# Part of the first tile's results that the adapters give: first half two row tiles on, second half behind the second tile's p7

## What is computed

```python
x = x + (x @ W.T + b + (x @ sign) * coeff)                # sign = 2*mask - 1, one matrix per batch
gate = x @ W_gate.T + 0.5 * (x @ A_gate[i].T) @ B_gate[i].T   # i: adapter of the batch
up   = x @ W_up.T   + 0.5 * (x @ A_up[i].T)   @ B_up[i].T
act  = silu(gate) * up
x = x + act @ W_down.T + 0.5 * (act @ A_down[i].T) @ B_down[i].T
```

## Time and profile before

| | us |
|---|---|
| median of 3 runs | 1600.77 |
| lowest and highest | 1599.63, 1600.84 |
| the profiled execution, its own time | 1599.98 |
| its span | 1598.2 |
| TensorE busy | 1557.8 (97%) |
| VectorE busy | 1219.1 (76%) |
| ScalarE busy | 803.0 (50%) |
| GpSimd busy | 355.3 (22%) |

### The profile page before, as it was taken

One profiled execution on the slowest core, in us unless ns is written; L12 is line 12 of the kernel. 1 busy time (PEld: TensorE's weight loads), 2 busy tenths in 40 slices (PEclk: granted clock), 3 DMA queues, 4 the chain that ended last, 5 costly groups with the idle time before them and its releaser, 6 DMA issues.

```text
span 1598.2 us, 23033 instructions
## 1 busy us (share of the span) xinstructions
PE 1557.8 (97%) x7508; PEld 1308.6 (82%) x7508; DVE 1219.1 (76%) x2134; ACT 803.0 (50%) x1478; POOL 355.3 (22%) x677
## 2 busy tenths in 40 slices
PE   6999998999999999999999989999999999999999
PEld 6999976888888888878888868888888888778887
DVE  8999877676666666688888877767666666788886
ACT  8999855444444444443334464444444444433332
POOL 0000131222222222253410012222212123543100
PEclk9999999999999999999999999999999999999999
DMA  9999853444444444698593724443444445996653
GB/s 371 373 363 364 302 177 125 139 138 155 143 136 155 155 155 155 224 352 270 182 370 111 239 83 155 155 144 122 151 151 143 133 152 175 337 343 209 224 192 118
DMA packets 137350, 325.24 MB, mean 204 GB/s; under 512 B 20112, under 2 KB 43792, under 8 KB 137232
## 3 DMA queue, kind: packets, MB, share of 16 engines
q0 software_dynamic: 56608, 175.81, 33.2%
q1 hardware_dynamic: 76016, 139.57, 25.8%
q10 hardware_dynamic: 4608, 8.39, 1.4%
HBM read 233.51 MB, written 90.18 MB: 203 GB/s over the span
## 4 chain that ended last, share of the span: by engine, by line
PE 90%; DVE 6%; issue 2%; ACT 1%; DMA 1%; POOL 0%; SPq 0%; DVEq 0%; POOLq 0%; ACTq 0%
PE ps L1447 60%; PE ps L1443 27%; PE ps L1571 2%; DVE acc L1088 1%; DVE op_b L1085 1%; DVE lo L1085 1%; DVE raw L1085 0%; DMA b_in<-in_b_gu 0%; DVE fx L1085 0%; DMA x_scratch<-x_out 0%; DMA ident_sb<-in_ident 0%; ACT t_gate L751 0%; POOL b_in L639 0%; DVE g L1088 0%; DVE raw L1088 0%
## 5 line engine op out<-in xcount | busy, mean ns | idle before, releaser
L1447 PE MATMUL ps<-op_b,hi 128*128 128x512 f32 x1616 | 500.8, 391 | 4.7 <-ACT ps L751 4.7
L1085 DVE TENSOR_TENSOR lo<-raw,hi 128x512 fp32r<-128x512 f32 (+2 forms) x640 | 332.7, 529 | 132.5 <-ACT hi L751 130.5
L751 ACT ACTIVATE hi<-raw 128x512 fp32r<-128x512 f32 (+1 forms) x592 | 304.5, 518 | 213.3 <-PE ps L1447 175.3
L1447 PEld LDWEIGHTS ps<-op_b,hi 128*128 128x128 f32 x1616 | 304.9, 189 | 70.4 <-ACT ps L751 5.6
L1447 PE MATMUL ps<-op_b,lo 128*128 128x512 f32 x808 | 316.8, 392 | 0.0
L1447 PE MATMUL ps<-op_d,hi 128*128 128x512 f32 x800 | 248.8, 392 | 8.5 <-DVE acc L1088 8.3
L1443 PE MATMUL ps<-op_b,hi 128*128 128x512 f32 x816 | 254.5, 393 | 0.0
L626 POOL DMA_DIRECT2D operand_scratch<-ot x140 | 75.7, 541 | 640.7 <-DVE ot L1085 605.7
L1088 DVE TENSOR_TENSOR acc<-acc,ps 128x512 f32<-128x512 f32 x248 | 169.7, 684 | 54.1 <-PE ps L1447 47.5
L1447 PEld LDWEIGHTS ps<-op_d,hi 128*128 128x128 f32 x800 | 147.8, 188 | 44.5 <-DVE acc L1088 14.3
L1443 PEld LDWEIGHTS ps<-op_b,hi 128*128 128x128 f32 x816 | 154.3, 189 | 33.7
(11 more groups left out here) (120 smaller groups left out, 2220.5 us busy)
## 6 DMA issues: line engine op xcount, KB each, us to landing
operand_scratch<-ot POOLq DMA_DIRECT2D x140, 512.0 KB, 3.9
op_d<-operand_scratch POOLq DMA_DIRECT2D x140, 512.0 KB, 10.8
raw<-in_wgu SPq DMA_DIRECT2D x168, 256.0 KB, 4.3
m_raw<-in_mask SPq DMA_DIRECT2D x64, 512.0 KB, 5.5
raw<-in_wd SPq DMA_DIRECT2D x160, 128.0 KB, 4.4
w_in<-in_w SPq DMA_DIRECT2D x32, 512.0 KB, 6.3
b_in<-in_b_gu POOLq DMA_DIRECT2D x264, 32.0 KB, 2.4
x_scratch<-x_out POOLq DMA_DIRECT2D x32, 256.0 KB, 4.8
```

The lines of the kernel that those rows point to most:

```text
L751: return nc.scalar.activation(o, i, ACT.Copy)
L1085: return nc.vector.tensor_tensor(o, a, b, ALU.subtract)
L1447: return mm(dst, weight, v, start=False, stop=stop, skip_group_check=True)
```

## The change

TensorE's order: r(0) moves from before h(1,4) to before h(1,6), and r(1) from before p3 of tile 1 to behind p7; td(0) moves from before p2 to behind it. The steps of ScalarE and VectorE follow: half 0's result comes after the first t4 form; t low of half 1 comes before the forms t3, `lora_b` of tile 1 goes out of `first_result` to the place before the last t3 form, and t neg goes behind the result. `lora_b` of tile 0 writes its weights into t_neg's tile (`b_first`), whose place is free until then, so that those of tile 1 need not wait for r. Both halves' gates use g1, with the counts of `silu_count` in the new order, and p3 of tile 1 waits for t_ready on TensorE by itself.

```diff
--- before.py
+++ after.py
@@ -71,17 +71,16 @@
             ("ta", 0, 1): a_part(0, 4) + forms("b22", 2, 3) + [("make", 0)],
             ("ta", 0, 3): a_part(0, 6) + [("make", 1)] + forms("t1", 0),
             ("ta", 0, 5): a_part(1, 0) + [("make", 2)] + forms("t1", 1),
-            ("ta", 0, 7): a_part(1, 2) + [("lora_b",), ("t sum", 0), ("make", 3)] + forms("t1", 2)
+            ("ta", 0, 7): a_part(1, 2) + [("lora_b", 0), ("t sum", 0), ("make", 3)] + forms("t1", 2)
                           + [("t own", 0), ("t high", 0), ("t low", 0)] + forms("t1", 3),
             ("ta", 1, 1): a_part(1, 4) + forms("t2", 0, 1, 2, 3),
             ("ta", 1, 3): a_part(1, 6),
+            ("h", 1, 5): [("make4", 0), ("make4", 1)] + forms("t4", 0),
             ("r", 0): [("result", 0)],
-            ("h", 1, 5): [("make4", 0), ("make4", 1)] + forms("t4", 0),
             ("h", 1, 6): [("make4", 2), ("make4", 3)] + forms("t4", 1, 2, 3),
             ("ta", 1, 7): [("t sum", 1)] + forms("t3", 0) + [("t own", 1)],
-            ("g", 1, "p1"): [("t high", 1)] + forms("t3", 1) + [("t low", 1)] + forms("t3", 2, 3),
-            ("r", 1): [("result", 1)],
-            ("g", 1, "p3"): [("t neg",)]}
+            ("g", 1, "p1"): [("t high", 1), ("t low", 1)] + forms("t3", 1, 2) + [("lora_b", 1)] + forms("t3", 3),
+            ("r", 1): [("result", 1), ("t neg",)]}
 
 
 def first_stage_order():
@@ -97,11 +96,10 @@
         for o in range(KQ, HT):
             order += [("h", s, 0, o)] + [("ta", s, 0, 2 * (o - KQ) + i) for i in range(2)]
         for o in range(HT):
-            if o == KQ:
+            if o == KQ + 2:
                 order += [("r", s, 0)]
             order += [("h", s, 1, o), ("ta", s, 1, o)]
-        order += [("g", s, 1, u) for u in PRODUCTS[:3]] + [("r", s, 1)]
-        order += [("g", s, 1, u) for u in PRODUCTS[3:5]] + [("td", s, 0)] + [("g", s, 1, u) for u in PRODUCTS[5:]]
+        order += [("g", s, 1, u) for u in PRODUCTS[:5]] + [("r", s, 1), ("g", s, 1, "p2"), ("td", s, 0), ("g", s, 1, "p4")]
         for f in range(2, PAIRS):
             order += [("g", s, f, u) for u in PRODUCTS[:4]] + [("td", s, f - 1)]
             order += [("g", s, f, u) for u in PRODUCTS[4:]]
@@ -272,6 +270,7 @@
                 t_gate = [sb(gate, f"t_gate{h}", [TR, N], f32r) for h in range(HALVES)]
                 t_up = [sb(gate, f"t_up{h}", [TR, N], f32r) for h in range(HALVES)]
                 t_neg = sb(gate, "t_neg", [TR, N], f32r)
+                b_first = t_neg[:, :].rearrange("p (a n) -> p a n", n=P)
                 b_w = sb(gate, "b_w", [TR, 2 * HALVES, P], f32r)
                 lw = sb(gate, "lw", [P, LW_RING, P], f32r)
                 b_in0 = sb(gate, "b_in0", [TR, 2 * HALVES, 2 * P], f32)
@@ -365,7 +364,8 @@
 
         def silu_count(s, f, half):
 
-            return s * (PAIRS * 2 + 2) + 2 * f + (1 + half if f in (0, PAIRS) else 2 - half)
+            turn = {(0, 1): 3, (1, 1): 2}.get((f, half), 2 * f + (1 + half if f in (0, PAIRS) else 2 - half))
+            return s * (PAIRS * 2 + 2) + turn
 
         a_count = silu_count
 
@@ -823,11 +823,9 @@
                 act.wait_ge(b_loaded[c % 2], 16 * 12 * b_turn(s, c))
                 if f > 1:
                     act.wait_ge(pe_done, done["g", s, f - 1, "p4"])
-                elif f:
-                    act.wait_ge(pe_done, done["r", s, 1])
-                elif s:
-                    act.wait_ge(pe_done, last_left(s - 1))
-                copy(b_w[:, :, :], b_in[c % 2][:, :, f % 2 * P:(f % 2 + 1) * P]).then_inc(bw_h, 1)
+                else:
+                    act.wait_ge(pe_done, done["h", s, 0, 0])
+                copy((b_w if f else b_first)[:, :, :], b_in[c % 2][:, :, f % 2 * P:(f % 2 + 1) * P]).then_inc(bw_h, 1)
 
             def prep(key):
                 if plan.slot_free[key]:
@@ -888,17 +886,13 @@
                     copy(dst[R2:2 * R2, :], u2[r:r + R2, :]).then_inc(t_hi, 1)
 
             def t_gu_neg(s):
+                act.wait_ge(pe_done, done["r", s, 1])
                 act.wait_ge(t_ready, 4 * s + 4)
                 nc.scalar.activation(t_neg[:, :], t_up[1][:, :], ACT.Copy, scale=-1.0).then_inc(t_neg_ready, 1)
 
             def first_result(s, half):
-                if half:
-                    lora_b(s, 1)
                 act.wait_ge(pe_done, done["r", s, half])
-                gate = (g1, g2)[half]
-                if half:
-                    act.wait_ge(t_ready, 4 * s + 4)
-                nc.scalar.activation(gate[:, :], first_bank(0, half)[:, :], ACT.Silu).then_inc(silu_made, 1)
+                nc.scalar.activation(g1[:, :], first_bank(0, half)[:, :], ACT.Silu).then_inc(silu_made, 1)
                 act.wait_ge(form_l, form_count(s, *(("t3", KQ - 1) if half else ("t1", 1))))
                 act.wait_ge(a_made, a_count(s, 0, half))
                 operand_hi((s, 0, ("b11", "b12")[half]), a32[:, half, :])
@@ -976,7 +970,7 @@
                             act.wait_ge(tm, tm_count(s, f // 2 - 1, name))
                             operand_hi((s, f // 2 - 1, name), src)
                 elif u == "p2":
-                    act.wait_ge(a_made, a_count(s, f - 1, 0))
+                    act.wait_ge(a_made, a_count(s, f - 1, int(f == 1)))
                     nc.scalar.activation(g1[:, :], ps[3 * (f % 2) + 2][:, :], ACT.Silu).then_inc(silu_made, 1)
                     act.wait_ge(a_made, a_count(s, f, 1))
                     operand_hi((s, f // 2, ("b12", "b22")[f % 2]), odd_or_even(f))
@@ -1050,7 +1044,7 @@
                     elif kind == "lw":
                         lora_a(("ta", s, *args))
                     elif kind == "lora_b":
-                        lora_b(s, 0)
+                        lora_b(s, *args)
                     elif kind == "t sum":
                         t_gu_sum(s, *args)
                     elif kind == "t own":
@@ -1150,8 +1144,8 @@
 
             def lora_b(s, f):
                 dve.wait_ge(bw_h, s * FT + f + 1)
-                q = slice(R2, 2 * R2)
-                sub(b_w[q, :, :], b_in[f // 2 % 2][q, :, f % 2 * P:(f % 2 + 1) * P], b_w[q, :, :]).then_inc(bw_l, 1)
+                q, tile = slice(R2, 2 * R2), b_w if f else b_first
+                sub(tile[q, :, :], b_in[f // 2 % 2][q, :, f % 2 * P:(f % 2 + 1) * P], tile[q, :, :]).then_inc(bw_l, 1)
 
             def raw_in(g, name):
                 cell, turn = plan.load_turn[g, name]
@@ -1225,11 +1219,10 @@
 
             def first_result(s, half):
                 if half:
-                    lora_b(s, 1)
                     dve.wait_ge(form_l, form_count(s, "t3", KQ - 1))
                 dve.wait_ge(pe_done, done["r", s, half])
                 dve.wait_ge(silu_made, silu_count(s, 0, half))
-                mult(a32[:, half, :], (g1, g2)[half][:, :], first_bank(1, half)[:, :]).then_inc(a_made, 1)
+                mult(a32[:, half, :], g1[:, :], first_bank(1, half)[:, :]).then_inc(a_made, 1)
                 operand_lo((s, 0, ("b11", "b12")[half]), a32[:, half, :])
                 if half:
                     dve.wait_ge(a_made, a_count(s, 0, 1))
@@ -1273,7 +1266,10 @@
                 elif u == "p3":
                     dve.wait_ge(pe_done, done[key])
                     dve.wait_ge(copied, copy_count(s, f, "p6"))
-                    dve.wait_ge(a_made, a_count(s, f - 1, int(f == 1)))
+                    if f == 1:
+                        dve.wait_ge(ta_own, 4 * (s + 1))
+                    else:
+                        dve.wait_ge(a_made, a_count(s, f - 1, 0))
                     add(g2[:, :], u2c[:, :], y_ps[:, :]).then_inc(c_made, 1)
                 elif u == "p7":
                     dve.wait_ge(pe_done, done[key])
@@ -1487,7 +1483,7 @@
                 pe.wait_ge(bw_l, s * FT + 1)
                 pe.wait_ge(t_ready, 4 * s + 2 * half + 2)
                 for row, t in enumerate((t_gate[half], t_up[half])):
-                    end = mm_on(first_bank(row, half)[:, :], b_w[:, 2 * half + row, :], t[:, :])
+                    end = mm_on(first_bank(row, half)[:, :], b_first[:, 2 * half + row, :], t[:, :])
                 end.then_inc(pe_done, 1)
 
             def gate_up(s, f, u):
@@ -1533,6 +1529,8 @@
                     mm_to(dst[:, :], high[:, w], op_b[:, i, :], start=first and k == 0)
                     mm_to(dst[:, :], high[:, w], op_b[:, i + 1, :])
                     if k == KQ - 1 and loras:
+                        if f == 1 and u == "p3":
+                            pe.wait_ge(t_ready, 4 * s + 4)
                         if u in ("p3", "q2"):
                             pe.wait_ge(bw_l, s * FT + f + 1)
                         if f == 1 and u == "p4":
```

## The result

| | us |
|---|---|
| before, median of 8 runs | 1601.35 |
| changed kernel, median of 8 runs | 1606.74 (1603.85 to 1607.59) |
| ratio to before | 1.0029, 95% interval 1.002 to 1.0038 |
| its profiled execution, its span | 1607.22, 1605.5 |

The change makes the kernel slower by 0.29% (about 4.6 us by the ratio, 5.4 by the medians, 7.2 in the two profiled executions). TensorE is busy 1557.8 us as before: it does the same work and waits more. In what follows a *fall* is a stretch in which TensorE's granted clock stands at 0.50 (1.2 GHz) instead of 1.00 (2.4 GHz).

The account below looks back on a forecast made before the run. TensorE, busy 97% of the span, was taken as the bound, so only its idle time and low-clock stretches could move. Block 0 +2.1, block 1 +1.25, one clock fall +1.6: together +4.9 us, 1605.7 us, range 1601.0 to 1608.5.

Parts of the forecast that it names:

- Part 1: r0 two row tiles later: its removed wait sat in front of a later one, before ta(1,6), so worth 0.0.
- +0.05 before p6: Block 0: r0's result now comes after the first t4 form, delaying what follows by 0.05 us, at most 0.2.
- Part 2: p3 takes r1's place, after p5's copy: -0.8 us in block 0, -0.9 to -2.4 in block 1, middle -1.65.
- Part 4: td0 behind p2 waits for its operand from r1, VectorE having p7's work queued ahead: 2.3 us in each block.
- Rival (a): td0's wait absent or a few tenths, if VectorE reaches r1's product before the two subtractions: 1598.7 to 1600.3 us; chance 0.15.
- One fall behind td0: Clock falls to half behind td0's new wait in one of the two blocks: +1.6 us, bounds 0 and 1.6 each.
- falls everywhere: High end of the forecast, with clock falls in both blocks: +7.3 us, 1608.1 us.
- Rival (b): Wait before ta(1,6) doesn't hold, so r0's waits and slow stretches are saved: -3.7 us, 1597.1 us; chance 0.08.

Follow-up runs that it names:

- r0_alone: The kernel before with only r(0) moved two row tiles later, to before h(1,6): 1601.42 us, ratio 1.0001.
- result_first: The changed kernel with half 1's result made ahead of the weights of tile 2's p5 on ScalarE and VectorE: 1598.82 us, ratio 0.9988.
- t2_late_again: Second run of the changed kernel with the four t2 forms behind ta(1,6)'s weight on VectorE: 1603.05 us, against 1606.56 for the changed kernel beside it.

## Why the prediction came out

It was right, in its time (1605.7 against 1606.74, inside 1601.0 to 1608.5) and in the steps of its mechanism; what was left loose was the clock. That its +4.9 us stand so near the measured 5.4 is in part luck. By the profiled executions, on which its sum was built, the change cost 7.2 us, and the sum was 2.3 short there: 1.6 for a second fall behind td0 and 0.75 for p3 in block 1. But the profiled execution of before (1599.98) lay 1.4 us under the median of 8 runs, where the prediction had added 0.8 from 3 runs, and that of the changed kernel only 0.5 above its own.

- **Part 1 (0.0).** Shown: ta(1,6) and p6 start where they did, r0_alone measures 1.0001. The waits of ta's weights were 2.47 and 2.10 us, forecast 2.7 and 2.4.
- **+0.05 before p6.** p6 at 245.79 instead of 245.70, put back: 0.09.
- **Part 2 (-0.8, -0.9 to -2.4).** p3 at 251.47, forecast 251.40, with the fall in it. In block 1 the middle, -1.65, was taken; the profiled execution had the fall and so the smaller gain, -0.9 (counted from ta(1,6): p3 ended at 954.61 - 2.90 = 951.71, forecast 951.6). The second execution of the changed kernel has 41.60 us there, 1.6 less: both ends occur.
- **Part 4 (2.3 us per block).** 2.19 and 2.18. The named cause, three instructions ahead of r1's product, is shown by result_first, which takes away 1.9 of them by order alone. Rival (a) was this kernel's cure and not its state.
- **One fall behind td0.** The term that was mis-sized: the profiled execution has one in each block, and so has the second one, so the distances give 3.7 and 3.8 us, against 3.7 and 3.6 for "falls everywhere". That sum, +7.3 us, is what the profiled executions differ by. The medians differ by 5.4; whether a typical run has fewer falls isn't shown, since 1.4 of the 1.8 us between the two figures are before's own.
- **Rival (b), faster,** fell with r0_alone and t2_late_again: no start of p6 or p3 moved. Its idea that the slow stretches are real losses holds, in these runs, only for those that no later wait covers.

Not settled: which executions get a fall, and where. It differs between executions of one kernel (43.16 and 41.60 us in block 1). Nor was td0 tried further back, behind p4, with VectorE's order left as it is.

## What to carry to other kernels

Before removing a wait, ask what the same engine meets next and whether the list behind that meeting started earlier: here two waits of one engine on one in-order queue were worth no more than the later one. Moving a consumer nearer to its producer uses up slack that is on no list of waits; count the distance against the producer's chain, with everything that is queued ahead of it, and if it doesn't fit, first look for work in the queue that isn't urgent. Here that order was worth 6.6 us by the ratios, more than the change itself cost.

## What the runs showed of the hardware

The clock of TensorE fell behind waits of 2.2 us (td0's in both blocks of the changed kernel) and 2.66 us, and not behind every such wait: not behind p6's 2.5 us in both blocks of it, and in r0_alone not even behind 3.21 us, where the granted clock is 1.00 from 228.72 to 232.13 (before, it was 0.50 behind 3.12 us). So in these traces the length of a wait alone doesn't tell whether a fall comes.

Eight and ten matmuls of no use inside the two waits went with a granted clock of 1.00 behind them and with 4.5 us less. Lengthening one wait to 4.9 us, so that the fall lay over a product with slack behind it, went with 3.5 us less, without any earlier start of p6 or p3.
